# Keys and values of a second attention made where they are used, in place of unread products

## What is computed

```python
def _L1_xattn(x, ctx, w_q, b_q, w_k, b_k, w_v, b_v, w_o, b_o):   # cut
    q = heads(norm(x) @ w_q + b_q)
    k, v = heads(ctx @ w_k + b_k), heads(ctx @ w_v + b_v)        # from the context alone
    a = softmax(q @ k.T / sqrt(16)) @ v                          # 8 batches, 16 heads
    return a.merge() @ w_o + b_o
# layer 0: the same with own keys beside the context's, a masked softmax, then a quantised gated block
# layer 1 ends in a mixture of 8 experts (two per row), weights 8 x (256 x 1024 + 1024 x 256)
```

## Time and profile before

| | |
|---|---|
| median of three runs | 618.8 us (612.36 to 625.53) |
| the profiled execution, its own time | 618.93 us |
| its span, first to last instruction | 617.2 us |
| mean granted TensorE clock | 0.893 |
| busy: PE, DVE, ACT, POOL | 80%, 69%, 49%, 26% |
| HBM read, written | 48.59 MB, 15.92 MB |

### The profile page before, as it was taken

How to read it: one execution, slowest core, us unless ns; L and a number is a source line. 1 busy time by engine, 2 the same in 40 slices (tenths; PEclk the granted TensorE clock), 3 DMA queues, 4 the chain that set the end, 5 groups by cost and what they waited for, 6 DMA issues and landing times. The chain is left out here.

```text
span 617.2 us, 15503 instructions
## 1 busy us (share of the span) xinstructions
PE 493.9 (80%) x5419; PEld 348.6 (56%) x5419; DVE 424.3 (69%) x920; ACT 302.2 (49%) x499; POOL 162.2 (26%) x191
## 2 busy tenths in 40 slices
PE   3987888898898877665478989999663299999993
PEld 2565566666565565333234656666443287887882
DVE  8767867777677754777528768877469776566651
ACT  5557565556555374143344757776542133333331
POOL 4600211221222111120245111101231425545432
PEclk9997999999999779786586989999775599999998
DMA  9577654454376000000467999994383012222210
GB/s 256 132 140 144 183 127 107 117 141 94 85 171 181 5 27 1 1 1 0 115 118 193 169 164 180 173 159 154 106 308 123 25 36 36 41 47 40 46 21 0
DMA packets 73247, 64.31 MB, mean 104 GB/s; under 512 B 33326, under 2 KB 65750, under 8 KB 73190
## 3 DMA queue, kind: packets, MB, share of 16 engines
q1 hardware_dynamic: 62904, 41.68, 31.3%
q0 software_dynamic: 8224, 21.06, 13.7%
q10 hardware_dynamic: 2064, 0.81, 0.5%
HBM read 48.59 MB, written 15.92 MB: 105 GB/s over the span
## 5 line engine op out<-in xcount | busy, mean ns | idle before, releaser
L518 PEld LDWEIGHTS PS<-QS,KS 112*120 112x120 f16 (+2 forms) x896 | 81.0, 140 | 28.8 <-issue 10.7
L518 PE MATMUL PS<-QS,KS 112*120 112x100 f16 (+2 forms) x896 | 89.2, 224 | 7.5 <-ACT QS L590 5.5
L629 DVE CUSTOM_DVE_ANT_0 PS<-PS,maskv 100x461 f32<-100x461 f32 x118 | 74.3, 647 | 14.7 <-PE PS L480 14.3
L632 DVE TENSOR_REDUCE mx<-PS 100x1 f32<-100x361 f32 x128 | 63.8, 529 | 30.0 <-PE PS L483 28.4
L581 ACT ACTIVATE PT<-PS 120x400 f32<-120x400 f32 (+1 forms) x128 | 63.3, 502 | 42.6 <-PE PS L518 41.5
L581 ACT ACTIVATE PT<-PS,ctxb 120x400 f32<-120x400 f32 (+1 forms) x96 | 56.9, 594 | 32.1 <-PE PS L518 30.9
L861 POOL TENSOR_SCALAR_AFFINE_SELECT PT<-PT 100x400 f32<-100x400 f32 x32 | 17.3, 541 | 159.9 <-ACT PT L581 159.9
L2173 PE MATMUL PS<-aT,WE 128*128 128x128 f16 x960 | 59.1, 223 | 0.0
L2173 PEld LDWEIGHTS PS<-aT,WE 128*128 x960 | 56.7, 100 | 0.1
L480 PE MATMUL PS<-KS,QS 65*100 65x461 f16 x118 | 44.9, 381 | 12.9 <-DVE mx L629 12.6
L2186 PE MATMUL PS<-WE,hidden_high 128*128 x160 | 53.0, 379 | 0.0
(11 more groups left out here) (322 smaller groups left out, 1050.2 us busy)
## 6 DMA issues: line engine op xcount, KB each, us to landing
share<-in_L_ffn_w_dram POOLq DMA_DIRECT2D x13, 1024.0 KB, 9.1
k_scratch<-share SPq DMA_DIRECT2D x32, 180.5 KB, 2.7
KS<-k_scratch SPq DMA_DIRECT2D x32, 180.5 KB, 3.9
KS<-k_scratch SPq DMA_DIRECT2D x64, 90.2 KB, 8.0
QS<-q_scratch SPq DMA_DIRECT2D x64, 50.0 KB, 2.8
v_scratch<-xn SPq DMA_DIRECT2D x8, 385.7 KB
values_staged<-v_scratch SPq DMA_DIRECT2D x8, 385.7 KB
WE<-in_L_ffn_w_dram POOLq DMA_DIRECT2D x2, 1024.0 KB, 8.7
```

The costliest lines, as they stand in the source:

```text
L518: last = nc.tensor.matmul(bank[0:kn, i * T:(i + 1) * T], KS[p][:, h, k0:k0 + kn], QS[p][:, h, :], start=True, stop=True)
L629: nc.vector.tensor_tensor_reduce(rows, rows, maskv[:, :], 1.0, -BIG, ALU.add, ALU.max, mx[p][:, h:h + 1]).then_inc(s_smf, 1)
L632: nc.vector.tensor_reduce(mx[p][:, h:h + 1], sm_bank[h % 2][0:T, 0:TC], X, ALU.max).then_inc(s_smf, 1)
```

## The change

Layer 1's keys and values no longer come from the first attention. There, each turned context (both halves, 370 KB) is written to DRAM instead; `pe_V` makes 256 columns for layer 0 alone, and key pieces 2 and 3 are gone. Only the keys of batches 0 and 1 are still made in the first block, in rounds 6 and 7 (steps 4, 5 and 1, 2), from contexts that are loaded back. In the second attention, round i makes the keys of batch i+2 (rounds 0 to 5) and the values of batch i+1 (rounds 0 to 6) on TensorE. SP loads each turned context twice, into `cK` and `cV`, writes the keys to DRAM, waits until they have landed and loads them back in the stacked layout. ACT copies values straight into place, without a bias: the bias of the values is added when the attention's outcome is turned (`act_attT`, `dve_attT`). Unread products remain in rounds 6 (8) and 7 (12), and 12 ahead of round 0. POOL's copies of values are gone.

```diff
-        TB, VB, KB, NB = (0, 2), (0, 1, 1), (0, 2, 0, 1), 2
+        TB, VB, KB = (0, 2), (0, 1, 1), (0, 2)
-        TVK = {1: "T0", 2: "T1", 4: "K0", 5: "K1", 8: "V0", 9: "V1", 11: "K2", 12: "K3"}
+        TVK = {1: "T0", 2: "T1", 4: "K0", 5: "K1", 8: "V0", 9: "V1"}
+        K17 = (1, 2)
...
-            nc.vector.tensor_tensor(V1s[p][0:kn, c, :, 0:DH], bank[:, 1], row[:, 1], ALU.add).then_inc(s_mf, 1)
...
+                sp.wait_ge(s_mf, N6)
+                sp.wait_ge(s_cw[0], 16 * B // 2)
+                sp_turned_in(sp, slice(0, 1), cT[0], s_c1)
...
+        K1T, K1H, K1L = (0, 4), (2, 5), (4, 10)
+        V1T, V1A, V1C = (6, 8, 9), (7, 10, 10), (2, 0, 1)
+        def pe_K1(pe, j, o, mb):
+            i = 2 * j + o
+            if mb == 0:
+                pe.wait_ge(s_ck, 16 * (i + 1))
+                pe.wait_ge(s_v1f, 3 * (i + 1))
+            else:
+                pe.wait_ge(s_k1f, 2 * i + 1)
+            pe_second_keys(pe, K1B, cK, mb).then_inc(s_k1d, 1)
+        def pe_V1(pe, i, q, behind_keys):
+            c = V1C[q]
+            if q == 0:
+                pe.wait_ge(s_cv, 16 * (i + 2))
+                if not (isinstance(i, int) and i < 0):
+                    pe.wait_ge(s_nm, 2 * i + 2 + 2 * B)
+            elif behind_keys:
+                pe.wait_ge(s_k1f, 2 * i + 2)
...
                 def round1(j, u, keys, nxt, more=True):          # SP
-                        for g in range(H // HG):
-                            sp.wait_ge(s_std, STN + NST1 * i + 3 * (g + 1))
-                            sp_keys1(sp, j, u + 2, g)
-                            if g % 2 == 1:
-                                sp_queries_in(sp, j, u + 2, g // 2)
+                        for mb in range(KC):
+                            sp.wait_ge(s_k1f, 2 * i + mb + 1)
+                            sp.dma_start(k_dram[1][bass.ds(i + 2, 1), mb * HM:(mb + 1) * HM, :, :, :].rearrange(
+                                "b h d s t -> (b h d) (s t)"), k1d[p][:, mb, :, :].rearrange("p s t -> p (s t)")
+                                ).then_inc(s_k1w[mb], 16)
+                            if mb == 1 and more:
+                                sp_turned_in(sp, bass.ds(i + 3, 1), cK, s_ck)
+                            sp.wait_ge(s_k1w[mb], 16 * (i + 1))
+                            if mb == 1:
+                                sp_queries_in(sp, j, u + 2, 0)
+                                sp.wait_ge(s_std, STN + NST1 * i + 9)
+                            sp_keys1(sp, j, u + 2, 2 * mb)
+                            sp.wait_ge(s_std, STN + NST1 * i + 6 * (mb + 1))
+                            sp_keys1(sp, j, u + 2, 2 * mb + 1)
+                        sp_queries_in(sp, j, u + 2, 1)
+                        sp.wait_ge(s_v1d, 3 * (i + 2))
+                        sp_turned_in(sp, bass.ds(i + 2, 1), cV, s_cv)
...
                 act.wait_ge(s_vz, 3)                             # ACT, ahead of the second biases
+                for q in range(3):
+                    act_V1(act, -1, 0, q)
...
-                for _ in range(24):                              # PE, ahead of round 0
+                for _ in range(12):
                     unread()
+                for q in range(3):
+                    pe_V1(pe, -1, q, False)
...
-                        unread()                                 # PE, each step
+                        if not keys and (not nxt or t < V1T[1]):
+                            unread()
+                        if keys and t in K1T:
+                            pe_K1(pe, j, o, K1T.index(t))
+                        if nxt and t in V1T:
+                            pe_V1(pe, 2 * j + o, V1T.index(t), keys)
```

More of the change, by code:

```diff
@@ L742, in _ @@
                 sp.wait_ge(s_mf, 4)
[L743 removed]
+                sp_keys_out(sp, 0, 0)
                 for mb in range(KC):
@@ L772, in round0 @@
                     p = u % 2
-                    if ctx or weights:
+                    if keys:
                         sp.wait_ge(s_mf, n0 + 2)
@@ L954, in round0 @@
                         act_exp(act, j, u, t, 0, 0)
+                        if nxt and not keys and kind_of(t)[:1] == "K":
+                            act_hi_K1b(act, 0, int(kind_of(t)[1]), N6 + int(kind_of(t)[1]))
+                        if weights and t in K17:
+                            act_hi_K1b(act, 1, K17.index(t), N7 + K17.index(t))
                         if t == NT2:
@@ L1216, in round0 @@
                     if nxt:
-                        dve_V(dve, j, u + 1, 2, n0 + (NW0 if keys else 2))
+                        dve_V(dve, j, u + 1, 2, nv + 2)
                 round0(0, 0, True, True, True)
@@ new lines, in flamingo, with act_hi_K1 @@
+        V1T, V1A, V1C = (6, 8, 9), (7, 10, 10), (2, 0, 1)
+        V1B = (misc[2][:, 0:D], misc[1][:, 0:D], misc[1][:, D:2 * D])
+        def pe_K1(pe, j, o, mb):
+            i = 2 * j + o
+            if mb == 0:
+                pe.wait_ge(s_ck, 16 * (i + 1))
+                pe.wait_ge(s_v1f, 3 * (i + 1))
+            else:
+                pe.wait_ge(s_k1f, 2 * i + 1)
+            pe_second_keys(pe, K1B, cK, mb).then_inc(s_k1d, 1)
+        def act_hi_K1(act, j, o, mb):
+            i, p = 2 * j + o, o % 2
+            if not (isinstance(i, int) and i == 0):
+                act.wait_ge(s_k1w[mb], 16 * i)
+            act.wait_ge(s_k1d, 2 * i + mb + 1)
+            nc.scalar.activation(k1d[p][:, mb, 0, :], K1B, ACT.Identity, bias=bcol[:, 3, mb:mb + 1]
+                                 ).then_inc(s_k1h, 1)
@@ L1783, in _, with round1 @@
                 act_max_rows(act, 0, 0, 0, 2 * B)
-                def round1(j, o, first, nxt, e, m, full):
+                def round1(j, o, first, keys, nxt, e, m, full):
                     for t in range(NST1):
@@ L1822, in _, with round1 @@
                 pe.wait_ge(s_wf, U["q1"] + 1)
-                for _ in range(24):
+                for _ in range(12):
                     unread()
+                for q in range(3):
+                    pe_V1(pe, -1, q, False)
                 for h in range(HA):
                     pe_SM(pe, 0, 0, h, 1, SMN)
+                pe.wait_ge(s_v1f, 1)
                 pe_N(pe, 0, 0, 0, SMN)
-                def round1(j, o, first, nxt):
+                def round1(j, o, first, keys, nxt):
                     h = HA
@@ L1833, in round1 @@
                         pe_ST(pe, j, o, t, 1, STN, 2 * B)
-                        unread()
+                        if not keys and t == 0:
+                            pe.wait_ge(s_v1f, 3 * (2 * j + o + 1))
+                        if not keys and (not nxt or t < V1T[1]):
+                            unread()
                         if not first:
```

358 lines of the change are left out of this document (212 added, 146 removed).

## The result

The changed kernel takes 635.99 us (median of 4 runs, 633.71 to 638.43) where the kernel before, beside it, takes 619.96 us: a ratio of 1.030, 95% interval 1.020 to 1.041. The forecast was 627 us in a range of 604 to 652.

A forecast was written before the change was run, and what follows sets the result against it. TensorE was taken to pace both attentions, with DMA half idle in the first and full in the second. 618.9 - 19 (first attention) + 27 (second attention) = 627 us, range 604 to 652.

The forecast's parts named there:

- SP's writes there change little: First attention: writing turned contexts (370 KB) for keys and values (361 + 386 KB), DMA at half load, costs nothing.
- First attention, steady: First attention, rounds 0 to 5: less TensorE work saves 3.0 us a round, 18 us (12 to 23).
- rival C: First attention gives less: maxima bound it, 2 us a round or less come back; 633 us, chance 0.13.
- Round 6: First attention, round 6: TensorE's key product waits for a context loaded back; 1 us (-1 to 4).
- TensorE in the second attention: Second attention, rounds with keys: unread products replaced by key and value products, 1.3 us more a round.
- ACT's two key and three value operations: Second attention: these added ACT operations, some 2.4 us a round, fit into its idle time at no cost.
- SP's chain: Second attention, rounds 1 to 5: SP's issues plus two 4.75 us landings make 18 us a round; +21.7 us.
- rival A: Second attention: writes land in 2.5 us, the waits are hidden, SP's queue keeps up; 608 us, chance 0.2.
- rival B: Second attention: landings take 6.6 us like the loads there, a round 21.7 us; 645 us, chance 0.27.
- Round 0 of the second attention: Second attention, first round: delayed expert load plus added TensorE work; +4.3 us.
- The bias chain: Second attention, first round: value copies delay ACT's bias scaling, POOL's bias operations and an expert load; 3 us (0 to 5.8).
- DMA has nothing to spare: Second attention: DMA share 1.03, engines full at 12.95 us; a 14 us round could hardly hold 715 KB more.

The follow-up runs named there:

- e1: Changed kernel with the writes of blocks 0 and 1's turned contexts issued before SP's wait for block 1's keys; 623.56 us, ratio 1.003.
- e2b: Changed kernel with contexts for the second layer's first keys loaded before round 4, the down weights' load waiting for the up weights; 632.86 us, ratio 1.026.
- e3: Changed kernel loading the first layer's keys in the second attention, so SP waits for no key landing; wrong keys; 628.66 us, ratio 1.014.
- e5: e4 with the next round's row maxima on ACT ahead of the two last value copies in the second attention; 629.68 us, ratio 1.018.
- e4: Changed kernel with e2b's loads and the second layer's keys made one round further ahead; 629.43 us, ratio 1.015.
- e9: e8 without the keys made one round further ahead and without the twelve added unread products; 620.07 us, ratio 1.004.
- e10: Changed kernel with expert step loads from the third on cut to one of 128 partitions; wrong expert weights; 630.44 us, ratio 1.019.
- e8: e7 with ACT's two scalings of the experts' second biases before the first block's three value copies; 610.52 us, ratio 0.986.
- e7: Changed kernel with e1, e2b's loads, e4, e5 and twelve more unread products before the second attention's first score rows; 617.38 us, ratio 0.995.

## Why the prediction came out where it did

The side was right and the range held. The time is 9 us over the forecast. The terms did worse than their sum: one was off by 12.6 us, and rounds 1 to 5 of either attention came out 3.5 and 3.7 us better than forecast, which hid part of it. That was luck.

- **The step that failed is a sentence**: "SP's writes there change little ... That costs and gives nothing." The bytes are indeed no matter. I weighed them as load and did not ask who waits for the write: the change has ACT wait for it from block 2 on (`s_cw`). In the steady loop it is free. At the loop's start, where the write is queued last, ACT waited 12.1 us for it, and the write issued sooner took 10.6 us off the round and 12.4 us off the time (e1). The changed kernel then takes 623.6 us.
- **First attention, steady.** I took 3.0 us a round between 2.0 and 3.8. It is 3.7: the maxima did not take it back, rival C is out. Ahead of the first round 4.6 against 3.
- **Round 6.** The wait is there as named; 1 us was too little, 2.6 is within the bounds. In e2b the round is 4.1 us shorter.
- **TensorE in the second attention.** 1.3 us a round, measured 13.63 - 12.51 = 1.1. Right.
- **"ACT's two key and three value operations ... fit into its 3.4 idle us."** They fit by sum and not by place. TensorE's waits for ACT, for the maxima and the outcome above all, rose from 0.2 us a round to 1.9 in e3, and the round is 15.8 us where I had 14.2. That the five operations ahead of them in ACT's order are the cause is shown for 0.5 us a round alone (e5); for the rest it is argued.
- **SP's chain.** The mechanism is shown (e3, e4, e9, e10), its size and law are not as I had them. A landing is not 4.75 us each time. In rounds 1 to 5 of the changed kernel the first write, issued 0.7 to 2.9 us behind a context load of the same queue and while a megabyte of expert weights was under way, lands in 3.0 to 6.0 us; the second, issued with no expert load under way, in 2.7 to 3.0. With 2 x 2.8, e10's median, the chain is an estimated 8.5 + 5.6 = 14.1 us, under the floor of 15.8, and costs nothing.

  What a round loses goes with the first landing: of the 20 rounds 1 to 5 of the four runs that wait for both (the changed kernel, e1, e2b, e9), the 8 in which it took up to 4.6 us last 15.2 to 16.0 us, the 12 in which it took 4.8 or more last 16.2 to 22.0. Those of 18 us and more are the ones in which the clock fell as well (0.91, in e2b's round 3 0.77). So rival A's short landing is right for a quiet queue and rival B's long one for a busy one. The average over rounds 1 to 5, 17.3 us, came near to my 18 by luck, from a higher floor and shorter waits. Round 6, 17.9 us, falls to 14.9 in e3 and e10.

  The Trainium skill (DMA: Bandwidth & Descriptors, Anatomy of one DMA) gives its fixed 2.0 us and 436 GB/s for DMAs that GpSimd issues; the 2.4 us estimated from them for such a write, which SP issues here, is near e10's 2.8 us. The Trainium skill (same page, Queues, rings and completion order) has an engine take turns between queues; the longer landings beside POOL's load agree.
- **Round 0 of the second attention.** 4.3 us predicted, 6.7 measured. The bias chain that I priced at 3 us (0 to 5.8) is the term that was too small: e8 shortens the round by 5.8 us against e7. In the changed kernel the expert load is issued 5.9 us behind the first score columns (324.71 us; 1.4 us before), and ACT waits 2.7 us for it. The half clock hides this: TensorE is busy for 20.15 of 22.15 us at 0.58, which is 11.7 us of work at full clock. But the clock alone does not set the round. All nine profiles with ACT's old order have ACT waiting 2.7 to 4.8 us for that load and a round of 22.2 to 24.3 us, at clocks from 0.53 to 0.77; e8 and e9, with the scalings first, have no such wait and take 17.4 and 18.6 us, e9 at 0.70 and without e6's products.
- **"DMA has nothing to spare."** The share of 1.03 that it rested on does not show it, and more bytes a microsecond went through in e3, see below. The sentence that a round of 14 us could hardly hold 715 KB more rested on it (697 KB in the profile's unit, in which a turned context has 361 KB); rounds of 15.2 to 15.8 us hold them, and no run has a shorter one that does.

e8 shows where a gain lay: in the same change, with its writes, loads and copies put where nobody waits for them. Its second attention still takes 120 us against 108; up to the end of the first, 22 us are gained.

## What to carry to other kernels

When a buffer that had only readers on chip is also written to memory, each reuse of it waits for that write: follow the write to its place in the queue at the loop's start, not only in the steady round. Work that fits into an engine's idle time by sum must still be placed: behind what the bound engine waits for, not ahead of it. The wait between a write and a load of the same data costs where the landing exceeds the chain's slack, so price its worst landing, beside the largest transfer of another queue; with the write made one round ahead it cost these rounds nothing (e4).

## What the runs showed of the hardware that I had not expected

- **A DMA share of 1.03 said little of the bytes.** The round of the earlier trace rows moved 187 GB/s at that share; in e3 the rounds 1 to 5 move 193 GB/s at 0.70, and key loads land in 3.0 us where they took 8.3. In the stretch of the earlier trace rows itself, the slices marked 9 moved between 116 and 371 GB/s:

```profile
GB/s 53 90 371 288 269 190 129 150 125 212 266 175 135 137 143 116 196 255 180 128 154 145 125 200 282 237 141 138 114 235 254 213 139 136 125 165 237 247 130 142
```

The share sums the time that packets took, and does not tell how many bytes still fit. What made the key loads slow before is not shown: the load of staged values, gone in the changed kernel, was not tried by itself.

- **Half clock with TensorE busy.** In the changed kernel, the stretch from 312 us to the first score columns, and then the rest of the half clock:

```profile
312.00:318.80 6.80, 4.72 (x11) 1.40 (x11) 5.72 (x11) 5.06 (x5) 4.36 (x1) 0.62 0.47 102
318.80:337.50 18.70, 17.80 (x127) 12.66 (x127) 9.56 (x17) 8.33 (x15) 7.22 (x4) 0.50 0.61 162
```

The clock fell to 1.2 GHz at 313.6 us, after TensorE had stood 2.2 us for queries (until 312.3) and 0.5 us for maxima (until 313.3). From the first score columns on it stayed there for another 18.7 us, in which TensorE was busy for 17.80. In the kernel before the same place had 10.2 us of half clock. What made it fall, and what would have brought it back sooner, is not shown.
